# A two-layer graph network: 112 sorted rows in place of 96, and a quarter of the sorted chunks summed during the first layer

## The reference, cut to what matters

```python
# layer 0, per edge:
msg   = silu(concat(h[src], h[dst], edge_feat) @ W1 + b1) @ W2 + b2
agg   = segment_sum(msg, dst, N)
h_new = silu(concat(h, agg) @ W3 + b3) @ W4 + b4
x     = layernorm(x + h_new + h)              # h = x: 2x + h_new
# layer 1:
agg   = segment_sum(x[src], dst, N)
z     = relu(((1 + eps) * x + agg) @ V1 + c1) @ V2 + c2
x     = layernorm(x + relu(layernorm(z + x) * gamma + beta))
```

## Time and profile before

| | us |
|---|---|
| median of 3 runs | 1622.17 (1622.05 to 1622.66) |
| the profiled execution | 1620.71 |
| its span, first to last instruction | 1618.8 |
| POOL busy | 1149.6 (71%) |
| PE busy | 1267.6 (78%) |
| DVE busy | 1013.1 (63%) |
| ACT busy | 631.5 (39%) |

### The profile page before, as it was taken

One profiled execution on the slowest core, in us unless ns is written; L12 is line 12 of the kernel. 1 busy time (PEld: TensorE's weight loads), 2 busy tenths in 40 slices (PEclk: granted clock), 3 DMA queues, 4 the chain that ended last, 5 costly groups with the idle time before them and its releaser, 6 DMA issues.

```text
span 1618.8 us, 31381 instructions
## 1 busy us (share of the span) xinstructions
PE 1267.6 (78%) x7946; PEld 1040.5 (64%) x7946; DVE 1013.1 (63%) x2298; ACT 631.5 (39%) x1272; POOL 1149.6 (71%) x1216
## 2 busy tenths in 40 slices
PE   4577777777777777777777877768999999999971
PEld 4455555556555655555565665558988888888861
DVE  6457777665756655454444445445678888888864
ACT  1335555555555555464555555201111111111111
POOL 4477777777777777777777777477777777777750
PEclk8889999999999999899999899879999999999985
DMA  4533333333333333533333333177677777777720
GB/s 123 152 77 94 94 96 93 91 92 94 93 92 93 92 92 92 91 99 91 99 87 97 92 91 92 43 236 215 190 205 219 218 217 219 218 217 218 220 67 24
DMA packets 187477, 207.44 MB, mean 128 GB/s; under 512 B 60410, under 2 KB 149437, under 8 KB 187395
## 3 DMA queue, kind: packets, MB, share of 16 engines
q1 hardware_dynamic: 134879, 122.15, 24.6%
q0 software_dynamic: 37888, 77.67, 19.6%
q10 hardware_dynamic: 14628, 6.68, 1.4%
HBM read 196.45 MB, written 9.82 MB: 127 GB/s over the span
## 4 chain that ended last, share of the span: by engine, by line
POOL 66%; issue 22%; PE 5%; DMA 4%; DVE 2%; DVEq 0%; SPq 0%; POOLq 0%; ACTq 0%; ACT 0%; PEldq 0%
POOL gath L739 66%; DMA xs<-in_x 1%; DMA out<-ot 1%; PE bank L1177 1%; DMA gath<-layer_input,src_col 1%; PE bank L1041 1%; PE bank L1164 1%; PE bank L1032 1%; DMA gath<-src_term,src_col 1%; PE bank L1149 1%; DMA dst_rows<-in_dst 1%; DVE st L1695 0%; PE bank L1028 0%; DVE ot L1711 0%; DVE nrm L1766 0%
## 5 line engine op out<-in xcount | busy, mean ns | idle before, releaser
L739 POOL DMA_INDIRECT gath<-src_term,src_col x784 | 740.9, 945 | 268.9 <-issue 237.7
L739 POOL DMA_INDIRECT gath<-layer_input,src_col x400 | 388.4, 971 | 125.1 <-issue 120.7
L1032 PE MATMUL bank<-gath,ident 128*128 128x512 f32 x392 | 233.7, 680 | 231.9 <-DMA gath<-src_term,src_col 231.3
L1384 DVE TENSOR_TENSOR oh<-bank,dst_rel 128x1024 f32<-128x1024 f32 x148 | 180.7, 1222 | 263.0 <-PE bank L1043 262.8
L1041 PEld LDWEIGHTS bank<-oh,msg 128*128 128x128 f32 x1568 | 224.3, 221 | 56.1 <-issue 55.6
L1638 DVE TENSOR_SCALAR_CACHE_REDUCE terms_l<-dst_bc,node_col 64x512 f32<-64x512 int32 x196 | 220.4, 1125 | 21.0 <-issue 10.2
L1028 PEld LDWEIGHTS bank<-terms_r,terms_l 128*128 128x128 f32 x1568 | 201.5, 194 | 49.5 <-issue 49.5
L1032 PEld LDWEIGHTS bank<-gath,ident 128*128 128x128 f32 x392 | 61.4, 197 | 260.9 <-DMA gath<-src_term,src_col 260.2
L1041 PE MATMUL bank<-oh,msg 128*128 128x128 f32 x1568 | 223.5, 304 | 0.0
L1028 PE MATMUL bank<-terms_r,terms_l 128*128 128x128 f32 x1568 | 210.0, 278 | 1.3 <-issue 1.3
L852 ACT ACTIVATE msg<-bank 128x512 f32<-128x512 f32 x196 | 115.7, 597 | 207.8 <-PE bank L1032 205.1
(11 more groups left out here) (179 smaller groups left out, 1554.2 us busy)
## 6 DMA issues: line engine op xcount, KB each, us to landing
dst_bc<-in_dst SPq DMA_DIRECT2D x195, 128.0 KB
xT<-sorted_src SPq DMA_DIRECT2D x48, 512.0 KB
gath<-src_term,src_col POOLq DMA_INDIRECT x784
terms_l<-layer_input SPq DMA_DIRECT2D x96, 128.0 KB
terms_r<-layer_input SPq DMA_DIRECT2D x96, 128.0 KB
msg<-layer_input SPq DMA_DIRECT2D x96, 128.0 KB
gath<-layer_input,src_col POOLq DMA_INDIRECT x400
ef_s<-in_edge_attr SPq DMA_DIRECT2D x97, 64.0 KB
```

The lines of the kernel that those rows point to most:

```text
L739: g.indirect_dma_start(out=gath[:, slot, j * D:(j + 1) * D], out_offset=None, in_=table[0:N, :], in_offset=bass.IndirectOffsetOnAxis(ap=in ...
L1032: mm(bank[h][:, :], ident[:, :], gath[:, slot, :], start=False, stop=True).then_inc(pre_ps, 1)
L1384: ve_.tensor_tensor(oh[:, u, :, :], iota_ps.unsqueeze(1).to_broadcast(shape), dst_rel[:, ds((k + first) * (2 * CH), 2 * CH)].unsqueeze(2). ...
```

## The change

ROWS is 112 and not 96: 56 pairs (14 blocks of 8 rows) are sorted and 42 pairs remain near. A block now has 4 octets of which the first (its 8 chunks of the lowest sources) is taken out of the second layer: its chunks need only the first 16 tiles of the first layer's output, and they are summed two chunks at a time ("early parts", 4 for a block, 56 in all) in steps 45 to 104 of the first layer. The second layer is left with 3 octets for each block, 42, and 42 near pairs. So that the sorted order is known by then, the sort goes three exchanges a step and not two, and ends in step 43 and not 62. In the second layer tiles go two at a time (24 units of two and one of one, placed by `tile_order`), the loops of that layer are written out, and in the first layer from tile 20 on, `out0` writes into bank 2, since bank 6 holds the early sums.

```diff
-ROWS = 96
+ROWS = 112
+EARLY_PART = 2
+EARLY_TILES = 16
...
+    BLOCK_OCTETS = BLOCK_ROWS * CH // OCT
+    LATE = BLOCK_OCTETS - 1
+    NOCT = NBLK * LATE
+    EARLY = NBLK * OCT // EARLY_PART
...
-        SORTED = 62
-        TURNS = (30, 31, 34, 35, 41, 42, 45, 46, 52, 53, 58, 59)
+        SORTED = 43
+        FIRST_EARLY = SORTED + 2
+        FIRST_BEFORE = (FIRST_EARLY + 3 - 8) // 2
...
+            units = [(LATE * b + 6, max(2 * b - 1, 0), 2 if b else 1, b, -1) for b in range(NBLK)]
+            units += [(4 * g + 10, SHARED + 2 * g, 2, -1, 4 * g + 7) for g in range((NT - SHARED) // 2 - 1)]
+            units += [(NEAR + 2, NT - 2, 2, -1, NEAR - 1), (NEAR + 4, SHARED - 2, 2, NBLK - 1, 3)]
...
 # SP, last stage of a step of the first layer
+            def load_early(e, m, q):
+                u = m % 2
+                first = q * BLOCK_OCTETS * OCT + m * EARLY_PART
+                sp.wait_ge(src_hot_made, done(2 * e - 3))
+                sp.dma_start(bc_early[:, u, :], rel_d[ds(first, EARLY_PART), :]...)
+                sp.wait_ge(rows_ps, done(e - 2))
+                load_windows(first, EARLY_PART, [...], x_near_in[u])
...
 # ACT, last stage of a step
+            def keep_early(e, m, q):
+                act.wait_ge(octet_ps, done(e - 2))
+                act.wait_ge(rows_ps, done(e))
+                a.copy(kept_early[:, m % 2, :, :], rows_early_ps...).then_inc(rows_kept_made, 1)
...
 # PE
+            def early_kept(e, m, q):
+                pe.wait_ge(rows_kept_made, done(e))
+            def hnew_read(j):
+                pe.wait_ge(v_made, done(j))
+            def early_rows(e, m, q):
+                pe.wait_ge(src_hot_made, done(2 * e + 1))
+                pe.wait_ge(x_near_in[u], 16 * EARLY_PART * (q * (STEPS // 2) + m // 2 + 1))
+                for c in range(EARLY_PART):
+                    for w in range(2):
+                        last = mm(rows_early_ps[:, c * D:(c + 1) * D], hot_early[...], near_early[:, u, c, w, :], ...)
+            def early_sums(e, m, q):
+                pe.wait_ge(rows_kept_made, done(e))
+                pe.wait_ge(dst_hot_made, done(e))
+                if m == 0:
+                    pe.wait_ge(v_made, done(FIRST_BEFORE - 1))
+                    pe.wait_ge(block_added, done(q - 1))
+                for c in range(EARLY_PART):
+                    last = mm(sums_early_ps, kept_early[:, u, c, :], dst_early[u][:, c, :], ...)
...
             steps(pe, NPAIR - 2, ...,
-                  of_pair(1, turn_ef), of_pair(2, pre_sums), (0, NPAIR, keys_taken), of_pair(3, message_sums),
-                  at_steps({4: weight_products}),
-                  of_unit(10, ordered_turn_x1), of_unit(8, out0), of_unit(7, ordered_hidden0),
+                  of_early(3, early_kept), of_pair(1, turn_ef), of_pair(2, pre_sums), (0, NPAIR, keys_taken),
+                  of_unit_in(FIRST_BEFORE, UNITS - 1, 9, hnew_read), of_pair(3, message_sums),
+                  at_steps({4: weight_products}), of_early(2, early_rows), of_early(3, early_sums),
+                  of_unit(10, ordered_turn_x1), *in_banks(8, ordered_out0), of_unit(7, ordered_hidden0),
...
 # DVE
+            def add_early(e, m, q):
+                if m == STEPS - 1:
+                    at = dve.value_load(block_base[0:1, ds(q, 1)], ...)
+                    dve.wait_ge(octet_ps, done(e))
+                    dve.wait_ge(block_added, done(q - 1))
+                    dve.wait_ge(T_init, done(2 * q + 2))
+                    ve_.tensor_tensor(T[:, ds(at, DW)], T[:, ds(at, DW)], sums_early_ps, ALU.add)...
+            def early_hots(e, m, q):
+                dve.wait_ge(src_bc_in[u], ...)
+                dve.wait_ge(rows_ps, done(e - 2))
+                source_hots(hot_early[:, u, :, :], bc_early[:, u, :])       # 2 x 128x256
+                dve.wait_ge(octet_ps, done(e - 2))
+                target_hots(dst_early[u], ..., EARLY_PART)                  # 128x576
...
-                elif 5 <= s < 23:
-                    in_rows(2 * (s - 5))
-                    in_rows(2 * (s - 5) + 1)
+                elif 5 <= s < 17:
+                    for n in range(3):
+                        in_rows(3 * (s - 5) + n)
...
             steps(dve, NPAIR - 2, ..., of_pair(1, windows), of_pair(1, one_hots(0, sums_ps, oh_made)),
-                  of_pair(3, add_sums), of_unit(9, ordered_norm0), (0, NPAIR, sort_edges))
+                  of_pair(3, add_sums), of_unit(9, ordered_norm0), (0, NPAIR, sort_edges),
+                  of_early(4, add_early), of_early(1, early_hots))
```

More of the change, by code:

```diff
@@ L419, in plain, with active @@
                         body(s - lag, (s - lag) % STEPS, (s - lag) // STEPS)
-            def whole(t):
+            def active(t):
                 first, last = t * STEPS, t * STEPS + STEPS - 1
-                return last < limit and not any(first <= s <= last for s in special) and \
-                    all(lag <= first and last - lag < count for lag, count, _ in stages)
+                inside = [lag <= first and last - lag < count for lag, count, _ in stages]
+                partly = [lag <= last and first - lag < count for lag, count, _ in stages]
+                whole = last < limit and inside == partly and not any(first <= s <= last for s in special)
+                return inside if whole else None
             t = 0
             while t * STEPS < total:
-                end = t
-                while whole(end):
+                end, inside = t, active(t)
+                while inside and active(end) == inside:
                     end += 1
@@ L433, in steps @@
                         for p in range(STEPS):
-                            for lag, count, body in stages:
-                                m = (p - lag) % STEPS
-                                body(q * STEPS + (p - lag), m, q + (p - lag - m) // STEPS)
+                            for run, (lag, count, body) in zip(inside, stages):
+                                if run:
+                                    m = (p - lag) % STEPS
+                                    body(q * STEPS + (p - lag), m, q + (p - lag - m) // STEPS)
                     t = end
@@ L512, in all_units1, with turn_of, reused, rows_of @@
                 for body in bodies:
-                    body(j, j, None)
+                    body(j, j, 1, None)
             for body in bodies:
-                body(UNITS - 1, UNITS - 1, None)
+                body(UNITS - 1, UNITS - 1, 2, None)
         def of_run(j, run):
             return j + run * UNITS
[L521 to L529, removed]
+        def turn_of(n, slot):
+            return n if slot is None else n // 2
+        def reused(n, slot):
+            return n - (1 if slot is None else 2)
+        def rows_of(first, count):
+            return ds(first * P, count * P)
+        def ends(first, count):
+            return isinstance(first, int) and first + count == NT
+        def stored(n, slot):
+            if slot is None:
+                return landed(n)
+            return landed(n + (1 if n >= ENDS else 0))
         def each_tile(eng, body):
@@ L639, in load_unit0, with load_unit1 @@
                     sp.dma_start(xt[0:rows, t, :], x[ds(tile * P, rows), :]).then_inc(xt_in, 16)
[L641 to L644, removed]
+            def load_unit1(n, first, count, slot):
+                sp.wait_ge(y_made, done(reused(n, slot)))
+                sp.dma_start(x1_rows[:, slot or 0, 0:count, :],
+                             x1_d[rows_of(first, count), :].rearrange("(t p) d -> p t d", t=count)) \
+                    .then_inc(x1_in[slot or 0], 16)
@@ L663, in load_octet @@
                              .to_broadcast([P, OCT * P])).then_inc(src_bc_in[u], 16)
[L664 to L669, removed]
+                sp.wait_ge(rows_ps, done(EARLY + 2 * o - 7))
@@ L859, in hidden0, with root @@
                 a.activation(hid[:, 0:n], bank[5][:, 0:n], ACT.Silu, bias=b3_col[:, :]).then_inc(hid_made, 1)
-            def root(n, j, made):
+            def root(n, count, made):
                 act.nop(nofuse=True)
-                a.activation(std[:, n, 0:tiles(j)], mv[:, n, 0:tiles(j), 1], ACT.Sqrt,
+                a.activation(std[:, n, 0:count], mv[:, n, 0:count, 1], ACT.Sqrt,
                              bias=eps_col[:, :]).then_inc(made, 1)
@@ L1196, in out1 @@
+            def out1(n, first, count, slot):
                 pe.wait_ge(z_made, done(n))
                 pe.wait_ge(r_made, done(n - 1))
-                for t in range(tiles(j)):
-                    at = place(t, parity, j) * P
-                    last = mm(bank[6][:, t * D:(t + 1) * D], hid[:, at:at + P], v2[:, :], start=True, stop=True)
+                for t in range(count):
+                    last = mm(bank[6][:, t * D:(t + 1) * D], hid1[:, slot or 0, t * P:(t + 1) * P], v2[:, :],
+                              start=True, stop=True)
```

503 lines of the change are left out of this document (293 added, 210 removed).

## The result

The changed kernel takes 1563.31 us (median of 4 runs, 1561.17 to 1566.61) against 1622.41 of the kernel before: a ratio of 0.9637, with a 95% interval of 0.9619 to 0.9655. That is 59 us faster. The forecast was 67 us (1555.6), and the range 1543 to 1580 holds the result.

A forecast was written before the change was run, and what follows sets the result against it. POOL's count of gathers was taken to set the time from 55 to 1565 us. Gathers -81.6, PE's early parts +6, turn +5, sort 0, tail +4 gave -66.6 us: 1555.6 us, range 1543 to 1580.

The forecast's parts named there:

- The gathers: Second layer on POOL: 8 near pairs, 64 gathers, go away at 1.276 us each; -81.6 us.
- PE in the stage with early parts: First layer, steps 45 to 100: PE's step grows to about level with POOL's 10.0 us; taken as 10.1, +6 us.
- the stall: First layer: PE's early sums wait 3.4 us for DVE's addition of the block before, every fourth step; 0.85 us a step.
- a clock at or above 0.95: Sign to look for on PE at 550 to 1000 us, as a busier PE would run nearer full clock.
- The turn: Between the layers: early parts 53 to 55 now lie there; 0 if hidden, 11 us in series, taken as +5.
- The tail: From the second layer's last gathered half pair to the end: 52.3 us becomes 56.5; +4 us, between -4 and +10.
- The sort at three exchanges: First layer's sort: DVE may fall 3 to 7 us behind, but POOL loses nothing; 0, or 7 us without cover.
- A: Rival: POOL keeps its pace everywhere, PE at 9.8 us a step, turn +2, tail 0; 1542.6 us, chance 0.19.
- B: Rival: PE bounds the first layer at 10.4 to 10.6 us a step; 1575 to 1586 us, chance 0.2.
- C: Rival: DVE's one-hot compares block POOL's gathers in the first layer, 10.4 us a step; 1571 us, chance 0.05.
- D: Rival: PE's step waits for ACT's late copy of the early rows, slower than before; 1639 us, chance 0.05.
- E: Rival: the counts send all engines to the any_order path, costing milliseconds; chance 0.01.

The follow-up runs named there:

- f1: On e1, SP also issues the load of the tile's rows (xt) one step earlier, ahead of the early part's loads; 1552.2 us.
- g3: f1 with half of PE's early products left out (odd sources, and each part's second chunk in the sums); 1548.5 us.
- e1: Changed kernel with DVE's early addition moved from the end of its step to the head; 1557.4 us.

## Why the prediction came out as it did

**The gathers.** -81.6 forecast, -79.4 measured. Right; the spacing grew from 1.276 to 1.282 us.

**PE in the stage with early parts: the term that was mis-sized.** "Sum for PE: 9.2 + 0.85 = 10.05 us a step", taken as 10.1 and +6 us, measured 10.23 a step. The end of the stage moved by 14.2, of which 11.9 are PE's lag and 2.3 are POOL's later start and end, which the sum put at nothing. By cycles of four steps: the sum had 40.2 us, and they take 40.9. PE's own step was put at 9.2 and is 8.8 without the stall, 1.6 too much in four; the wait was put at 3.4 and is 3.7; and the lower clock behind it, some 2 us in each long step, was not in the sum at all. So two errors of opposite sign nearly cancelled, and that the range held owes something to luck. I had argued the other way, from the mean clock, that a busier PE would run faster, and named "a clock at or above 0.95" as the sign: it is 0.93 against 0.94 before. What counts is the one long wait in four steps; with the addition moved the clock is 0.99, with the stall filled 1.00. Besides, the late `xt` costs PE 0.7 us in one of the short steps; I had put it into DVE's slack and had not asked whether PE waits for `rows0`, as it now does by `hnew_read`.

**The turn.** +5 forecast, +6.4 measured. The forecast hid about half of what it listed; the trace of the changed kernel shows nearly all of it in series. Between the last `message_sums` and the last L1906 (L1731 before), 12.2 us where it was 5.4, PE does three early parts, some 6 us, and waits 1.05 us for DVE's early sum and 2.25 for `hnew_read`; gone from that path is DVE's own wait for `xt`, 3.0 us in the kernel before. The runs price only two of these: half of the early products are 2.0 us (f1 and g3), and the late `xt` with the clock behind it 4.1 us once the addition is moved (e1 and f1). How they share the 6.4 of the changed kernel stays open.

**The tail.** +4 forecast, +2.4 measured. Stores of two tiles came 7.2 us apart (forecast 7.3):

```profile
1536.59 0.38 ACTq L1011 DMA_DIRECT2D out<-ot  x1
...
1543.78 0.38 ACTq L1011 DMA_DIRECT2D out<-ot  x1
```

**The sort at three exchanges.** Right at 0: the `message_sums` of pairs up to 440 us come at most some 4 us behind those of the kernel before, and the gap is 0 again in between. The profile names PE ahead of 21 of POOL's gathers in the first layer, but none of these gaps is longer than the 0.3 us between any two: POOL does not stand.

**The rivals.** A (POOL keeps its pace) needed the stall to vanish; with that and the load moved, the time is 1552, still some 10 us over its 1543. B named what happened, PE as the bound of the first layer, at a smaller price: it had 10.4 to 10.6 a step, and for a reason, gaps at each new wait, that the short steps of 8.66 us exclude. C is excluded as a price: 361 gathers start in 450 us as before, one at 946 ns and not 944 in this stretch, with two compares a step beside them. Single gathers do show it. This one starts inside the two compares:

```profile
699.03 0.61 DVE L1837 TENSOR_SCALAR xTs<-As,even_odd 128x256 f32<-128x256 f32 x2
699.44 1.02 POOL L831 DMA_INDIRECT gath<-src_term,src_col  x1 [0.30 <-issue]
```

Of 352 gathers between 594 and 1034 us 12 take over 0.96 us, 11 of them beside such a compare, and in the kernel before 2 of 353 do; the mean spacing goes from 1.249 to 1.251 us, under 1 us over the whole stage. The Trainium skill ("SBUF — State Buffer", who interferes with whom) states an exclusive lock; a hold-up of some gathers, 0.13 us at most, agrees with it and does not prove it. D and E did not occur.

## What to carry to other kernels

When an edit adds a wait on the engine that is nearly the bound, count the wait and then what the clock takes behind it, and look first for the same work at another place of the other engine's step: what DVE adds here was ready on PE a step earlier, and one moved line took the wait away. A transfer that moves behind another one's wait on the same queue must be followed to its last reader, also through waits that the same edit adds. And a shorter main stage is worth its time only if what trails it fits: here the tail is 46 us longer with one tile a unit than with two.

## What was unexpected of the hardware

A wait of 3.7 us in PE's stream made its step 5.8 us longer: for some 5 us behind it the granted clock was 0.50, and 8 instructions took 1.85 us where they take 1.05. Filling the wait with unused products took 2.4 us off. The mean granted clock of a stage (0.93 against 0.94 before) hid that; the rows just behind the wait show it. And 36 GB/s more of window loads (129 against 93) came with gathers of 946 ns in place of 944.
